# Query and key strips placed by transfers through memory instead of selection products

## What is computed

```
x = x + attn(cond(x, itok, cond_weight, cond_bias), W_Q, W_K, W_V, W_o)
x = x + moe(lora_ffn(x, itok, wi, wo, ...), w1, b1, w2, b2, w3, b3, gate_w, gate_b)

def attn(x):                       # 16 heads, d_head 16, causal
    Q, K, V = heads(x @ W_Q), heads(x @ W_K), heads(x @ W_V)
    scores = Q K^T / 4 + causal
    return (softmax(scores) V) @ W_o
```

## Time and profile before

| | us |
|---|---|
| median of 3 runs (1393.32 to 1398.42) | 1396.8 |
| the profiled execution | 1383.05 |
| its span, first to last instruction | 1380.4 |
| TensorE busy | 1267.0 |
| VectorE busy | 799.0 |
| ScalarE busy | 641.5 |
| GpSimd busy | 609.5 |

### The profile page before, as it was taken

One profiled execution on the slowest core, in us unless ns is written; L12 is line 12 of the kernel. 1 busy time (PEld: TensorE's weight loads), 2 busy tenths in 40 slices (PEclk: granted clock), 3 DMA queues, 4 the chain that ended last, 5 costly groups with the idle time before them and its releaser, 6 DMA issues.

```text
span 1380.4 us, 26539 instructions
## 1 busy us (share of the span) xinstructions
PE 1267.0 (92%) x8129; PEld 944.5 (68%) x8130; DVE 799.0 (58%) x1845; ACT 641.5 (46%) x1230; POOL 609.5 (44%) x929
## 2 busy tenths in 40 slices
PE   5888999999999999999999885598999999999997
PEld 3545666666666666657566565387888888888886
DVE  3564665766667667756756644254555555555553
ACT  4364564564654655655645620133343333333332
POOL 3333443444463553554634644242535444444442
PEclk9579999999999999999999998699999999999999
DMA  7112313313334444343233385368252225352210
GB/s 282 62 46 77 135 53 118 120 47 132 103 69 109 109 79 126 96 108 118 72 77 120 62 134 88 116 217 304 42 173 46 39 38 174 57 162 35 40 26 11
DMA packets 57805, 138.78 MB, mean 101 GB/s; under 512 B 13283, under 2 KB 35302, under 8 KB 56434
## 3 DMA queue, kind: packets, MB, share of 16 engines
q0 software_dynamic: 31072, 67.47, 20.0%
q1 hardware_dynamic: 26658, 70.32, 16.8%
HBM read 88.20 MB, written 51.54 MB: 101 GB/s over the span
## 4 chain that ended last, share of the span: by engine, by line
PE 71%; DMA 9%; DVE 7%; ACT 6%; issue 4%; POOL 3%; POOLq 0%; SPq 0%; DVEq 0%; ACTq 0%
PE bank L715 66%; DMA xg<-hrows,gid 4%; PE bank L999 4%; DVE nmax L1431 3%; DMA w_rest<-in_w_all 3%; ACT probs_t L1175 2%; ACT q_sb L1182 2%; PE bank L991 1%; DMA wsplit<-w_rest 1%; POOL id_table L1642 1%; POOL w_rest L1625 1%; PE bank L932 0%; ACT ot_sb L1191 0%; PE bank L925 0%; DMA id_table<-route_sb,slot_id 0%
## 5 line engine op out<-in xcount | busy, mean ns | idle before, releaser
L1431 DVE TENSOR_REDUCE nmax<-bank 128x1 f32<-128x512 f32 (+3 forms) x512 | 221.3, 484 | 109.1 <-PE bank L715 107.7
L1175 ACT ACTIVATE probs_t<-bank 128x512 f32<-128x512 f32 (+1 forms) x384 | 181.1, 525 | 115.5 <-PE bank L715 115.1
L1213 ACT ACTIVATE g<-z 128x512 f32<-128x512 f32 x142 | 89.8, 632 | 280.8 <-DVE z L1557 280.8
L715 PE MATMUL bank<-wst,g1t_high 128*128 x568 | 184.6, 406 | 0.9 <-DVE g1t_low L1542 0.9
L1695 POOL DMA_INDIRECT out<-y_sb,sid x71 | 114.3, 1609 | 147.1 <-DVE y_sb L1578 61.4
L1606 POOL TENSOR_SCALAR_AFFINE_SELECT probs_t<-probs_t 128x256 f32<-128x256 f32 x256 | 98.1, 410 | 169.3 <-ACT probs_t L1175 168.8
L1557 DVE TENSOR_TENSOR z<-bank,b_sb 128x512 f32<-128x512 f32 x142 | 98.2, 692 | 73.4 <-PE bank L715 62.8
L715 PEld LDWEIGHTS bank<-wst,g1t_high 128*128 128x128 f32 x568 | 102.9, 191 | 20.1 <-issue 1.1
L715 PE MATMUL bank<-q_sb,k_sb 64*128 64x512 f32 (+3 forms) x512 | 91.9, 393 | 25.1 <-ACT probs_t L1175 15.8
L715 PE MATMUL bank<-wst,g1t_low 128*128 x284 | 112.9, 398 | 0.0
L715 PE MATMUL bank<-wst,g2t_high 128*128 x568 | 110.3, 292 | 1.5 <-DVE g2t_low L1542 1.5
(11 more groups left out here) (209 smaller groups left out, 2882.0 us busy)
## 6 DMA issues: line engine op xcount, KB each, us to landing
wst<-wsplit SPq DMA_DIRECT2D x8, 4096.0 KB
w_rest<-in_w_all POOLq DMA_DIRECT2D x64, 256.0 KB, 3.0
wsplit<-w_high POOLq DMA_DIRECT2D x64, 256.0 KB
wsplit<-w_rest POOLq DMA_DIRECT2D x64, 256.0 KB
hrows<-h_sb SPq DMA_DIRECT2D x8, 528.0 KB, 7.5
x_in<-in_xT SPq DMA_DIRECT2D x8, 512.0 KB, 4.6
wb_raw<-in_lora_wb SPq DMA_DIRECT2D x8, 512.0 KB, 3.6
x1t<-in_xT SPq DMA_DIRECT2D x8, 512.0 KB, 5.2
```

The costliest lines, as they stand in the source:

```text
L715: return nc.tensor.matmul(*a, **k)
L1175: taken(nc.scalar.activation(probs_t[:, (2 * g + half) % PT_SLOTS, S * u:S * u + width], at(n, rd)[:, 0:width], ACT.Exp), n, rd)
L1213: nc.scalar.activation(g[:, :], z[:, :], ACT.Gelu).then_inc(s_g, 1)
L1431: ins = V.tensor_reduce(nmax[:, g % 2, half, i:i + 1], at(n, rd)[:, cols], AX.X, ALU.max, negate=True)
```

## The change

Both halves of the heads (`BY_DMA = (0, 1)`) get their strips by transfers. SyncE stores q's two parts and k's two parts of a half to `part_rows` in memory (512 KB each), waits until both have landed, and issues 12 loads, each of 16 rows by 4 pairs by 512 columns (128 KB), into the blocks of the strips, and 2 loads of zeros into rows 32 and 33 of `q_sb`. All 16 selection products' banks and their evictions fall away. The parts of `q_sb` and `k_sb` that no transfer writes are cleared once by GpSimd at the start (k's ones too). TensorE's first score of a half waits for that half's 14 loads; ScalarE's eviction of hid 0 waits for all 4 stores of the round, for `hid_high` lies over `parts`. hid 0 and v 1 change places. The diff, without the declarations of semaphores and what only renames the point of round 0 at which constants are prepared:

```diff
@@ -64,6 +64,7 @@
 W_PIECES = W_ALL // W_PIECE
 W_SLOTS = 3
 PV_BANK = 6
+BY_DMA = (0, 1)
 
 PAIRS = HEADS // 2
 QUADS = PAIRS // 2
@@ -98,6 +99,7 @@
 
 TAIL_STEP = PAIRS * CHUNKS + 1
 PT_SLOTS = 6
+STRIP_LOADS = 2 * 2 * 3 + 2
 BEHIND = 8
 
 
@@ -149,7 +151,8 @@
     quads = [[(w, 4 * c + pair) for pair in range(4)] for c in range(KD) for w in ("qs", "ks")]
     order = [("x1t", 0), ("x1t", 1)] if feeds else [("cond", o) for o in range(KD)] + list(LED[0:2])
     order += ([] if feeds else list(LED[2:])) + [("k", 1), ("v", 0)]
-    order += quads[0] + [("low_i", 0)] + quads[1] + [("hid", 0), ("v", 1)] + quads[2] + [("hid", 1)] + quads[3]
+    quads = [[n for n in quad if n[1] // 4 not in BY_DMA] for quad in quads]
+    order += quads[0] + [("low_i", 0)] + quads[1] + [("v", 1), ("hid", 0)] + quads[2] + [("hid", 1)] + quads[3]
     order += [("hid", j) for j in range(2, HID_EARLY)]
     ours = ("cond", "q", "k", "v", "qs", "ks")
     return [n for n in order if (attends if n[0] in ours else feeds)]
@@ -233,6 +236,8 @@
                  gate_w, gate_b, w_all, b1, b2, b3, ident, maskd, tri, sel, marks, route_c,
                  tile_c, pads, out):
     hrows = nc.dram_tensor("hrows", [B * S, ROW], F32, kind="Internal").ap()
+    part_rows = nc.dram_tensor("part_rows", [2, KD, 2, P, S], F32, kind="Internal").ap()
+    zeros = nc.dram_tensor("zeros", [2, 4, S], F32, kind="Internal").ap()
     id_table = nc.dram_tensor("id_table", [NE * CAP, 1], F32, kind="Internal").ap()
     wsplit = nc.dram_tensor("wsplit", [NE, P, 2, W_ALL], F32, kind="Internal").ap()
     out_rows = out.rearrange("b s d -> (b s) d")
...
@@ -605,9 +615,38 @@
                 sp.dma_start(wst[:, (1 - r) % W_SLOTS, :, :].bitcast(F32),
                              wsplit[r:r + 1, :, :, :].rearrange("o p h n -> (o p) h n")).then_inc(s_w, 16)
 
+            def strips(rd, c):
+
+                for w, what in enumerate("qk"):
+                    if rd.p is not None and (what, c) in LED:
+                        drained(sp, ("l" + what, c), Round(rd.p))
+                    else:
+                        drained(sp, (what, c), rd)
+                    sp.dma_start(part_rows[w, c, :, :, :].rearrange("i p t -> p i t"),
+                                 parts[:, c, 2 * w:2 * w + 2, :].bitcast(F32)).then_inc(s_parts_out, 16)
+                if rd.p is None and c == BY_DMA[0]:
+                    sp.wait_ge(s_cleared, 1)
+                    sp.dma_start(zeros, q_sb[M_ROW + 2:M_ROW + 4, 4 * c:4 * c + 4, :].bitcast(F32)).then_inc(s_zeros, 16)
+                    sp.wait_ge(s_zeros, 16)
+                sp.wait_ge(s_parts_out, 16 * 2 * (len(BY_DMA) * rd.b + BY_DMA.index(c) + 1))
+                for w, (to, blocks) in enumerate(((q_sb, (0, 1, None, 0)), (k_sb, (0, 0, None, 1)))):
+                    for half in range(2):
+                        for blk, part in enumerate(blocks):
+                            if part is not None:
+                                rows = slice(STRIP * half + DH * blk, STRIP * half + DH * (blk + 1))
+                                sp.dma_start(to[rows, 4 * c:4 * c + 4, :].bitcast(F32),
+                                             part_rows[w, c, part, :, :].rearrange("(g h d) t -> h d g t", h=2, d=DH)[half]
+                                             ).then_inc(s_strips[c], 16)
+                for half in range(2):
+                    rows = slice(STRIP * half + M_ROW, STRIP * half + M_ROW + 2)
+                    sp.dma_start(q_sb[rows, 4 * c:4 * c + 4, :].bitcast(F32), zeros).then_inc(s_strips[c], 16)
+
             def turn(rd, last=False):
+                if rd.b is not None:
+                    for c in BY_DMA:
+                        strips(rd, c)
                 if rd.b is None:
-                    filled(sp, ("ks", HEADS // 2 - 1), Round(rd.p))
+                    filled(sp, ("hid", HID_EARLY - 1), Round(rd.p))
                     sp.dma_start(tile_sb[:, :], tile_c).then_inc(s_tile_c, 16)
                     filled(sp, ("pv", QUADS - 1), Round(rd.p))
                     load_run(0)
...
@@ -879,7 +918,9 @@
                     score, late, m, quad, norm, scale = work_at(step)
                     if score is not None:
                         g, u = score
-                        if u == 0:
+                        if u == 0 and g // 4 in BY_DMA:
+                            pe.wait_ge(s_strips[g // 4], 16 * STRIP_LOADS * (b + 1))
+                        elif u == 0:
                             drained(pe, ("qs", g), rd)
                             drained(pe, ("ks", g), rd)
                         for half in range(2):
@@ -1119,6 +1160,8 @@
                     return
                 elif what == "hid" and piece in (None, KD - 1):
                     filled(act, n, rd)
+                    if m == 0 and b is not None:
+                        act.wait_ge(s_parts_out, 16 * 2 * len(BY_DMA) * (b + 1))
                     nc.scalar.activation(hid_high[:, m, :], at(n, rd)[:, :], ACT.Relu).then_inc(s_hid_high, 1)
                     return
                 elif what == "bo":
...
@@ -1596,6 +1640,19 @@
             nc.gpsimd.memset(ones_b[:, :], 1.0)
             nc.gpsimd.memset(v_sb[:, :, :, :, 1, :].rearrange("p t k c d -> p (t k c) d"), 1.0).then_inc(s_vzero, 1)
 
+            blank, ones = probs_t[:, 0, 0:S], probs_t[:, 0, S:2 * S]
+            nc.gpsimd.memset(probs_t[:, 0, 0:2 * S], 0.0).then_inc(s_clearing, 1)
+            pool.wait_ge(s_clearing, 1)
+            for half in range(2):
+                ins = nc.gpsimd.memset(ones[STRIP * half + M_ROW:STRIP * half + M_ROW + 2, :], 1.0)
+            ins.then_inc(s_clearing, 1)
+            pool.wait_ge(s_clearing, 2)
+            for c in BY_DMA:
+                pairs = slice(4 * c, 4 * c + 4)
+                nc.gpsimd.tensor_copy(q_sb[:, pairs, :], blank.unsqueeze(1).to_broadcast([P, 4, S]))
+                ins = nc.gpsimd.tensor_copy(k_sb[:, pairs, :], ones.unsqueeze(1).to_broadcast([P, 4, S]))
+            ins.then_inc(s_cleared, 1)
+
             def allowed(rd, g, u, tiles):
 
                 drained(pool, ("st", g, u, 1), rd)
```

More of the change, by code:

```diff
@@ L438, in build_kernel @@
         s_hi = sem("s_hi")
+        s_clearing = sem("s_clearing")
+        s_zeros = sem("s_zeros")
+        s_cleared = sem("s_cleared")
+        s_parts_out = sem("s_parts_out")
+        s_strips = [sem(f"s_strips{c}") for c in range(KD)]
         s_mhigh = sem("s_mhigh")
@@ L867, in turn @@
                         pe.wait_ge(s_idb, 1)
-                    if p is None and n == ("qs", 0):
+                    if p is None and n == ("v", 0):
                         pe.wait_ge(s_sel, 1)
@@ L1153, in turn @@
                         nc.scalar.copy(wv_high[:, :, :], wv_raw[:, :, :]).then_inc(s_prep_high, 1)
-                    if p is None and n == ("qs", 0):
+                    if p is None and n == ("v", 0):
+                        act.wait_ge(s_cleared, 1)
                         act.wait_ge(s_sel_f, 32)
```

## The result

The kernel with transfers takes 1509.1 us in the median of its runs (1502.8 to 1514.9), the one before 1397.6 on the same chip: a ratio of 1.081, interval 1.078 to 1.085. Slower was forecast, but by 75 us instead of 112. Ratios in this document go by the fast executions alone, medians by all: one of e1_half is 2% slower than the others at a lower clock, and c2_before_body and e9_half_body had one each of 2368 and 6529 us, for which nothing here gives a cause.

What follows compares the result with a forecast made beforehand. TensorE bounds it, busy 1267.0 of 1380.4 us. Rounds 2 to 7 +59, round 1 +6, round 0 +10: +75 us, 1458 profiled, 1472 in the median; 8 in 10 between 1410 and 1505.

Steps and rivals of the forecast that it cites:

- What goes: Opening: 256 selection products and a 0.78 us gap fall away; TensorE gains 3.7 us a round, at most 30 us.
- Waits in the opening: TensorE's first score waits for c = 0's loads, ScalarE's first relu for all four stores, bg for VectorE's hid_low.
- Stores landed: Rounds 2 to 7: c = 0's two stores landed at H+9.4 (5.9 to 12.9), H being the hrows store's issue.
- Loads: SyncE's twelve 16-row loads per half: 1.1 us each, 13.2 us, plus 1 us to land; in place at H+23.6.
- The estimate from the Trainium skill: 16 rows reach four of 16 SBUF ports: 1.2 us a load, twelve 14.5, total about +86, 1483 us.
- Opening, rounds 2 to 7: Bank 3 drained at H+27.8 against bg at H+21.0: 6.8 us late a round, the 3.7 us gain already in it.
- The clock: After TensorE idles some 10.5 of 11 us, a lower clock slows its products: 3 us a round added.
- The body: The rest of a round after the opening was to stay near 78 us.
- rival D: c = 1's loads delay GpSimd's weight pieces, masks and pv products, 2 us in each of 8 rounds: 1488 us; 7%.
- Rounds 0 and 1: Round 0's first score late, strips at 43.2 against 33.26, +10 us; round 1, with no hrows before it, +6.1.

Runs made afterwards that it cites:

- e1_half: Changed kernel with only the second half of the heads by transfers, the first half by selection products as before: 1412.6 us against 1384.7, 1.020.
- c2_before_body: Kernel before, with GpSimd's weight pieces moved out of the opening, one loaded ahead of each pair's masks and split behind them: 1542.1 us, 1.101.
- e9_half_body: Second half of the heads by transfers, with GpSimd's weight pieces moved out of the opening into the body: 1540.4 us, 1.100 to the kernel before.
- e7_no_loads: Changed kernel without the 24 part loads of a round, stores and small loads of zeros kept: 1391.7 us, 0.997 to the kernel before.
- e10_half_small: Second half of the heads by transfers, GpSimd's weight pieces moving 16 columns from the ninth on: 1380.3 us against 1399.6, 0.984.
- e2_wide: Changed kernel with each load into 128 rows by 256 columns instead of 16 rows by 2048, same bytes: 1414.1 us, 1.023 to the kernel before.
- e4b_busy: Changed kernel with 36 unused products added on TensorE at the end of each opening, rounds 1 to 7: 1497.9 us, 1.085 to the kernel before.
- ref_after: Changed kernel unaltered, run again on another chip beside other runs: 1503.4 us, 1.088 to the kernel before.
- e6_small_pieces: Changed kernel with GpSimd's weight pieces moving 16 columns instead of 512 from the ninth on: 1450.1 us, 1.050 to the kernel before.
- c1_before_small: Kernel before, with GpSimd's weight pieces moving 16 columns instead of 512 from the ninth on: 1407.3 us, 1.006.

## Why the prediction was wrong

- **What goes: right.** Where transfers hold the opening little or not at all (e7_no_loads, e1_half, e10_half_small), bg comes at H+17.8 to 19.5 against H+21.0: 3.2 us of the forecast 3.7 in the quiet rounds of e7_no_loads, and 1.5 to 2.8 where half of the selection products are left.
- **Waits in the opening: right in kind and place.** First score for the strips, relu for the stores, bg for hid_low, all three in the rows above.
- **Stores landed: H+5.6, 6.4, 11.1, 11.8, 10.9, 11.1.** The mean, 9.5, is the forecast's 9.4. One value for all was too plain: rounds 2 and 3 are like round 1's quiet case, those with scattered writes are 1.8 later than forecast.
- **Loads: nearly right.** From the first load's issue to the first score 15.6, 16.0, 15.1, 16.3, 14.4 and 15.3 us, 15.5 in the mean, against 14.2: less 1 us to land, 1.2 us each, not 1.1. The earlier trace rows pointed the other way, and the deciding argument was 8 KB to each of 16 rows; e2_wide confirms it by spreading them. The estimate from the Trainium skill (SBUF — State Buffer, Door 1: The DMA port swizzle), 1.2 us a load, agrees with this. No run varied which rows a load reaches at an equal count, so that ports rather than rows are the reason isn't shown here.
- **Opening, rounds 2 to 7: 50 us against 41.** The relu starts at H+28.0 in the mean, forecast 26.4.
- **The clock: right that it falls, wrong that this fills the body's account.** 3 us a round were charged. Half clock behind the opening is in the rows (0.55 in round 2), but taking half of it away (e4b_busy) shortened the six bodies by 6 us and the total by 5.5.
- **The body: this is the step that failed.** It was to stay near 78 us, with the clock as its whole cost (18 us in six rounds); in the sum the delay of GpSimd's pieces was put at nothing and left to rival D at 7%, with 16 us. The six bodies took 47 us more, 84.6 in the mean against 76.8, and TensorE waited 24.5 us for masks. Emptying the pieces gives back 53 us: 31 in these bodies, 21 in the openings. So the term that was missing is the meeting of the pieces with the strips' transfers. The mechanism of D is the right one, and its price, 2 us a round, was under half of the 5 that the bodies alone give back. D named c = 1's loads as the cause; the chain below shows c = 0's at work as well. D left out the other direction: the pieces also hold up the strips' stores and loads, 3.5 us an opening.
- **Rounds 0 and 1: 27 us against 16.** Round 0's first score is 11.3 late (forecast 10), and 5.5 more are lost in its body; round 1's opening fits (5.7), its body loses 4.8.

How the failed step works is seen in GpSimd's own chain in the first part of round 3 (H is 356.84): part of the chain of waits from 360 to 420, start and length.

```profile
364.72 6.85 DMA w_rest<-in_w_all
...
374.44 8.03 DMA wsplit<-w_rest
...
382.76 4.21 DMA w_rest<-in_w_all
...
389.82 10.91 DMA wsplit<-w_rest
...
401.02 5.66 DMA w_rest<-in_w_all
```

Load a piece, split it, store it, only then the next: each transfer is in GpSimd's program order, so each extra microsecond of landing is its own. GpSimd's waits over the first 64 us of round 3, opening and half of the body, before (318 to 382):

```profile
POOL probs_t L1606 <- ACT probs_t L1175: 14.1, 7, 5.1
POOL w_high L1623 <- DMA w_rest<-in_w_all: 13.1, 5, 3.3
POOL w_rest L1616 <- DMA wsplit<-w_rest: 8.0, 3, 3.2
```

and after (356 to 420):

```profile
POOL w_rest L1673 <- DMA wsplit<-w_rest: 24.3, 4, 10.6
POOL w_high L1680 <- DMA w_rest<-in_w_all: 18.6, 5, 6.4
```

Before, GpSimd reached the masks early and waited 14.1 us for ScalarE's probabilities: that was the cover. After, it waits 42.9 us for its pieces to land instead of 21.1, the first row is gone, and the next in line, TensorE's pv products (probabilities times values), have to wait for the mask. Over the whole run the two landing waits grew from 224 to 404 us, and GpSimd's waits for ScalarE fell from 169 to 105. The cover of some 14 us in this round could have been read from the trace before; in TensorE's waits, where GpSimd stood with 0.6 us, it doesn't show.

The full ledger by experiment, of the 121 us between ref_after and the kernel before it: pieces against strips 53; the narrow form of the loads some 90, which holds most of these 53 too, for with spread loads small pieces change the ratio only from 1.023 to 1.014, some 12 us; stores, loads and relu in series 20, with neither, after what the missing products give. Taken singly they overlap, so they don't add up.

**What stays open.** The body's 47 us aren't split cleanly between clock and masks: in e6_small_pieces both the waits for masks and half of the time at half clock are gone, and how much the clock costs once no mask is waited for was not tried. The 47 us are also counted against a short execution of the kernel before (1383.05, median 1396.8): the bodies of c1_before_small, which moves no strip, take 478.0 us, 17 more than its 461.0, with 41 us at half clock in rounds 2 to 7 against 10. Nor is it settled whether two buffers for the pieces would restore the cover with the transfers in place; that was not tried, there being no room for a second buffer. No kernel that does all of the work was faster than the one before.

## What to carry to other kernels

Ask of every transfer how many SBUF rows it reaches, not only how many bytes it has: twelve loads of 128 KB into 16 rows filled the DMA engines' time for some 15 us, and the same bytes into 128 rows were in place after 9 to 10. Then look for every other engine that waits for its own transfers in program order, and read its slack from its waits for others, not from TensorE's waits for it; that slack is what new traffic uses up first. A test with half of the change told more than the whole one: the opening got faster and the kernel slower, which pointed at once to something outside the opening.

## What the hardware showed that was not expected

- Loads of 16 rows: 141 GB/s at a DMA share of 1.09, against 256 GB/s at 0.89 for the same bytes in 128 rows. In the changed kernel's own trace stores out of 128 rows moved 392 GB/s at a share of 1.05 (249 to 252.5). DMA share alone doesn't tell that bandwidth is used; read it beside GB/s.
- Such loads also slow what goes to other places at the time: GpSimd's 256 KB pieces landed in 5.0 us in the median instead of 3.0, and one store of its pieces held it for 10.9.
- Halving the time at half clock, from 133 to 65 us, moved the median by 5.5 us while TensorE's waits for GpSimd were there. Whether products at half speed merely fill time that would be a wait isn't shown.
- Some 20 us of gain were hidden in the half version and show at 0.984 only with the pieces small: TensorE's waits for an engine that is 44% busy, 32.0 us, cost more than the 128 products that this version takes out, half of the 23.4 us in the earlier trace rows.
